# Attention and expert mixture on one core: inverse row sums of 24 spans split in two, transposed together with the row maxima one slot later, and spread to the heads' rows by a 0/1 product

## The reference, cut to what matters

```python
x = x + xattn(layernorm(x), ctx, ctx, ...)     # 16 query heads, 4 key heads, causal, 4 batches of 512 tokens
x = x + ffn(layernorm(x), ...)                 # router, top 4 of 128, 8 basis units, 2 shared units

# inside xattn
scores = einsum('bgnqd,bgkd->bgnqk', qg, k) * scale
scores = where(causal, scores, -1e30)
attn   = softmax(scores)                       # row maximum, exponential, row sum
out    = einsum('bgnqk,bgkd->bgnqd', attn, v)
```

## Time and profile before

| | |
|---|---|
| median of 3 runs | 805.96 us (805.74 to 808.08) |
| the profiled execution | 808.76 us, its span 807.0 us |
| mean granted TensorE clock over the span | 0.985 |
| TensorE busy | 764.5 us, 95% of the span |
| VectorE, ScalarE, GpSimd busy | 648.7, 575.9, 534.8 us |

### The profile page before, as it was taken

How to read it: one execution, slowest core, us unless ns; L and a number is a source line. 1 busy time by engine, 2 the same in 40 slices (tenths; PEclk the granted TensorE clock), 3 DMA queues, 4 the chain that set the end, 5 groups by cost and what they waited for, 6 DMA issues and landing times. The chain is left out here.

```text
span 807.0 us, 15292 instructions
## 1 busy us (share of the span) xinstructions
PE 764.5 (95%) x4180; PEld 607.6 (75%) x4180; DVE 648.7 (80%) x1639; ACT 575.9 (71%) x1409; POOL 534.8 (66%) x685
## 2 busy tenths in 40 slices
PE   2769799999999999999999999999999999999998
PEld 2546577777777878877778778787778887788886
DVE  7767987889788877889789787898788887688774
ACT  3878797788777867788778767787777775655552
POOL 5585689784697769775687859776565615662572
PEclk9977999999999999999999999999999999999999
DMA  8322144554545446645455445554545335454650
GB/s 292 124 67 89 42 140 162 177 168 138 194 161 173 147 141 223 191 152 180 147 174 179 141 154 181 172 166 139 199 152 172 129 127 185 157 186 132 207 203 34
DMA packets 57052, 127.03 MB, mean 157 GB/s; under 512 B 10920, under 2 KB 28040, under 8 KB 56968
## 3 DMA queue, kind: packets, MB, share of 16 engines
q1 hardware_dynamic: 56968, 126.04, 47.3%
HBM read 107.55 MB, written 4.46 MB: 139 GB/s over the span
## 5 line engine op out<-in xcount | busy, mean ns | idle before, releaser
L1656 PE MATMUL u<-w_h,t_h 128*128 128x512 f32 x640 | 257.8, 403 | 0.7 <-issue 0.5
L1656 PE MATMUL u<-w_l,t_h 128*128 128x512 f32 x640 | 250.5, 391 | 0.0
L1656 PE MATMUL u<-w_h,t_l 128*128 128x512 f32 x640 | 250.4, 391 | 0.0
L1296 DVE TENSOR_TENSOR w_l<-w_raw,w_h 128x512 fp32r<-128x512 f32 x288 | 242.3, 868 | 0.3 <-ACT w_h L956 0.3
L956 ACT ACTIVATE w_h<-w_raw 128x512 fp32r<-128x512 f32 x380 | 216.8, 621 | 8.5 <-DMA w_raw<-in_w_units 7.4
L910 POOL TENSOR_TENSOR w_l<-w_raw,w_h 128x512 fp32r<-128x512 f32 x96 | 139.4, 1452 | 96.5 <-ACT w_h L956 96.4
L991 ACT ACTIVATE scores<-scores,mx 128x384 f32<-128x384 f32 (+1 forms) x224 | 128.8, 575 | 72.9 <-DVE mx L1239 71.7
L918 POOL TENSOR_TENSOR macc<-macc,gb 128x256 f32<-128x256 f32 x112 | 106.6, 955 | 58.4 <-DVE gb L1403 58.1
L1239 DVE CUSTOM_DVE_ANT_0 scores<-s,mask_qk 128x384 f32<-128x384 f32 (+1 forms) x224 | 112.4, 503 | 35.9 <-PE s L1532 34.8
L1656 PEld LDWEIGHTS u<-w_h,t_l 128*128 128x128 f32 x640 | 120.2, 188 | 27.0
L1656 PEld LDWEIGHTS u<-w_h,t_h 128*128 128x128 f32 x640 | 120.6, 188 | 25.7 <-issue 2.7
(11 more groups left out here) (153 smaller groups left out, 1180.8 us busy)
## 6 DMA issues: line engine op xcount, KB each, us to landing
w_raw<-in_w_units SPq DMA_DIRECT2D x160, 512.0 KB, 4.2
w_raw<-in_w_out_t SPq DMA_DIRECT2D x16, 512.0 KB, 5.2
w_raw<-in_shared_w_down SPq DMA_DIRECT2D x16, 512.0 KB, 4.6
q_st<-turned_h SPq DMA_DIRECT2D x224, 32.0 KB, 2.9
out<-x SPq DMA_DIRECT2D x16, 256.0 KB, 2.3
q_st<-turned_l SPq DMA_DIRECT2D x112, 32.0 KB, 2.8
x<-in_x SPq DMA_DIRECT2D x3, 1024.0 KB, 9.2
k_st<-turned_h SPq DMA_DIRECT2D x48, 32.0 KB, 2.8
```

Source lines behind the costliest of these rows:

```text
L1296: e.tensor_tensor(w_l[:, i % WR, k, :], w_raw[:, i % WR, k, :], f32(w_h[:, i % WR, k, :]), ALU.subtract).then_inc(s_wl, 1)
L1656: last = e.matmul(u_bank[n % 2][:], t[:, k, cols], ww[:, i % WR, k, :], start=(k == 0 and m == 0), stop=(k == KC - 1 and m == 2))
```

## The change

For spans 8 to 31 the 8 inverse sums of a row are no longer copied 32 times and transposed as 128x128 blocks. GpSimd splits them into a high and a low part (two instructions on 128x8) beside the maxima's parts in `mhl`, which becomes 16 wide. `maxima_turn` then turns maxima and inverse sums together; it becomes two ordinary products in the rounded 32-bit format with the identity (for spans 4 to 7 too, maxima alone). For spans 8 to 31 it moves from the end of slot S to slot S+1, behind the first product of `pass_a`, and waits for GpSimd's split; `maxima_out` and `rows` move to S+1 too. `inverse_turn` becomes one product of 256 columns, a 128x128 matrix of zeros and ones ("chooser") times `m_t`, and moves from S+5 to S+3. GpSimd's split is the first work of its slot S+1; VectorE inverts earlier in slot S, behind the eviction of the last filler. The chooser is made once by GpSimd in slot 52, in the place that `rrep` had.

```diff
+INVERSE_ROWS, CHOOSER_SLOT, MAXIMA_LATER = 3, 52, 1
...
+    SPREAD = H * KV
...
-        mhl, m_t = sb("mhl", [P, 2, TH, 2 * G], F32R), sb("m_t", [2 * G, Q], F32R)
-        rrep, r_t = sb("rrep", [P, TH, P]), sb("r_t", [P, 2, Q])
+        mhl, m_t = sb("mhl", [P, 2, TH, 4 * G], F32R), sb("m_t", [P, Q], F32R)
+        with ExitStack() as before:
+            rrep = before.enter_context(nc.sbuf_tensor("rrep", [P, TH, P], F32))
+        chooser, r_t = sb("chooser", [P, TH, P], F32R), sb("r_t", [P, 2, Q])
...
             for u in range(KV, NU):
-                if s == span_slot(u) + CORE[name]:
+                if s == span_slot(u) + CORE[name] + (MAXIMA_LATER if name == "maxima" and u >= SPREAD else 0):
                     return u
...
-            return u if u is not None and (u < H * KV) == first else None
+            return u if u is not None and (u < SPREAD or MAXIMA_LATER > 0) == first else None
...
+        def inverse_parts(u):
+            return s_isplit, 4 + 2 * (u - SPREAD + 1)
...
+        def inverse_rows_in(s):
+            for u in range(SPREAD, NU):
+                if s == span_slot(u):
+                    return u
+            return None
+
+        def inverse_turn_in(s):
             for u in range(NU):
-                if s == span_slot(u) + core(u, name):
+                if s == span_slot(u) + (core(u, "inverse_turn") if u < SPREAD else INVERSE_ROWS):
                     return u
...
+            def inverse_split(u):
+                r = u % 2
+                hi, lo = (mhl[:, r, :, i * G:(i + 1) * G] for i in range(2))
+                e.wait_ge(s_rinv, u + 1)
+                if u >= KV + 2:
+                    e.wait_ge(s_mt, u - KV - 1)
+                e.tensor_copy(hi, rinv[:, r]).then_inc(s_isplit, 1)
+                e.wait_ge(s_isplit, inverse_parts(u)[1] - 1)
+                e.tensor_tensor(lo, rinv[:, r], f32(hi), ALU.subtract).then_inc(s_isplit, 1)
+            def make_chooser():
+                e.wait_ge(s_rt1, SPREAD)
+                rows = chooser[:, 0, :]
+                e.memset(f32(rows), 0.0).then_inc(s_isplit, 1)
...
+                e.affine_select(out=by_head(rows), in_=by_head(f32(rows)), compare_op=ALU.not_equal, fill=1.0, base=0,
...
+                e.affine_select(out=by_head(rows), in_=by_head(f32(rows)), compare_op=ALU.not_equal, fill=1.0, base=-G,
...
             for s in slots:
+                if (u := inverse_rows_in(s - 1)) is not None:
+                    inverse_split(u)
                 if (step := second_pass_step(s - SELECT)) is not None:
                     mask_probabilities(*step)
                 if (hb := of_half(s, "query_scale")) is not None:
                     query_scale(hb)
-                if (u := of_span(s, "spread")) is not None:
+                if s == CHOOSER_SLOT:
+                    make_chooser()
+                if (u := of_spread_span(s, "spread")) is not None:
                     spread_inverse(u)
...
+                if u > SPREAD:
+                    e.wait_ge(s_rt1, u)
+                made = 2 * G if u < SPREAD else 4 * G
+                e.activation(m_t[0:made, :], short("maxima", u - KV)[0:made, 0:Q], ACT.Copy).then_inc(s_mout, 1)
...
             def maxima_turn(u):
                 e.wait_ge(s_mlo, u - KV + 1)
+                if u >= SPREAD:
+                    e.wait_ge(*inverse_parts(u))
+                first = 2 * G if u < SPREAD else 0
                 e.wait_ge(*short_free("maxima", u - KV))
                 bank = short("maxima", u - KV)
                 for t in range(TH):
-                    last = e.transpose(bank[0:2 * G, t * P:(t + 1) * P], f32(mhl[:, u % 2, t, :]), ident[:])
+                    last = e.matmul(bank[0:4 * G - first, t * P:(t + 1) * P], mhl[:, u % 2, t, first:4 * G], ident_r[:],
+                                    start=True, stop=True)
                 last.then_inc(s_mt, 1)
 
             def inverse_turn(u):
 
+                if u >= SPREAD:
+                    e.wait_ge(s_mout, u - KV + 1)
+                    e.wait_ge(*short_free("inverse", u))
+                    e.matmul(short("inverse", u)[:, 0:Q], chooser[:, 0, :], m_t[:],
+                             start=True, stop=True).then_inc(s_rt1, 1)
+                    return
```

More of the change, by code:

```diff
@@ L706, in rows @@
                     e.wait_ge(*queries_read(u - QR))
+                first = 0 if u < SPREAD else 2 * G
                 for k in range(2):
                     e.dma_start(f32(q_st[MAXROW + k:MAXROW + k + 1, u % QR, :, :]),
-                                f32(m_t[k * G:(k + 1) * G, :])).then_inc(s_m[u % 2], 16)
+                                f32(m_t[first + k * G:first + (k + 1) * G, :])).then_inc(s_m[u % 2], 16)
             def store(g):
@@ L773, in pool_engine @@
             e.memset(half_neg[:], -0.5).then_inc(s_small, 1)
-            e.memset(ident[:], 0.0)
+            e.memset(f32(m_t[:]), 0.0).then_inc(s_isplit, 1)
+            e.memset(ident, 0.0)
             e.memset(lg[:, :, :, NE:NE + 8], -1.0)
@@ L982, in maxima_out @@
                     e.wait_ge(*max_rows(u - 1))
-                e.activation(m_t[:], short("maxima", u - KV)[0:2 * G, 0:Q], ACT.Copy).then_inc(s_mout, 1)
+                if u == KV:
+                    e.wait_ge(s_isplit, 1)
+                if u > SPREAD:
+                    e.wait_ge(s_rt1, u)
+                made = 2 * G if u < SPREAD else 4 * G
+                e.activation(m_t[0:made, :], short("maxima", u - KV)[0:made, 0:Q], ACT.Copy).then_inc(s_mout, 1)
             def row_sum(u, m):
@@ L1438, in vector_engine @@
                     mixture_table()
+                if (u := inverse_rows_in(s)) is not None:
+                    inverse(u)
                 for u, m in first_pass_tiles(s)[1:]:
@@ L1491, in turn_in @@
                 for t in range(TH):
-                    last = e.transpose(bank[:, t * P:(t + 1) * P], r1_b[:, n % 2, t, :], ident[:])
+                    last = e.transpose(bank[:, t * P:(t + 1) * P], r1_b[:, n % 2, t, :], ident)
                 last.then_inc(s_turn, 1)
@@ L1503, in turn_stacked @@
                             copies = r3[:, n % 2, t * G + 2 * i + j].rearrange("p c d -> p (c d)")
-                            last = e.transpose(stack_banks(n)[i][0:MAXROW, j * Q + t * P:j * Q + (t + 1) * P], copies, ident[:])
+                            last = e.transpose(stack_banks(n)[i][0:MAXROW, j * Q + t * P:j * Q + (t + 1) * P], copies, ident)
                     last.then_inc(done, 1)
@@ L1520, in inverse_turn @@
                 for t in range(TH):
-                    last = e.transpose(bank[:, t * P:(t + 1) * P], rrep[:, t, :], ident[:])
+                    last = e.transpose(bank[:, t * P:(t + 1) * P], rrep[:, t, :], ident)
                 last.then_inc(s_rt1, 1)
@@ L1542, in turn_probabilities @@
                         at = j * w + t * P - seen(u, k)
-                        last = e.transpose(pair[:, at:at + P], masked_scores(u, j * TH + t)[:, k * P:(k + 1) * P], ident[:])
+                        last = e.transpose(pair[:, at:at + P], masked_scores(u, j * TH + t)[:, k * P:(k + 1) * P], ident)
                 last.then_inc(s_pb, 1)
@@ L1579, in turn_x @@
                 for k in range(KC):
-                    last = e.transpose(bank[:, k * P:(k + 1) * P], xn[:, k * P:(k + 1) * P], ident[:])
+                    last = e.transpose(bank[:, k * P:(k + 1) * P], xn[:, k * P:(k + 1) * P], ident)
                 last.then_inc(s_xt, 1)
@@ L1599, in turn_choice @@
                 for t in range(2):
-                    last = e.transpose(bank[:, t * P:(t + 1) * P], cf[:, t, 0:NE], ident[:])
+                    last = e.transpose(bank[:, t * P:(t + 1) * P], cf[:, t, 0:NE], ident)
                 last.then_inc(s_cft, 1)
@@ L1622, in turn_down @@
                     for k in range(ND // 2):
-                        last = e.transpose(bank[:, k * P:(k + 1) * P], blocks[h * (ND // 2) + k], ident[:])
+                        last = e.transpose(bank[:, k * P:(k + 1) * P], blocks[h * (ND // 2) + k], ident)
                     last.then_inc(s_dt, 1)
```

37 lines of the change are left out of this document (25 added, 12 removed).

## The result

The changed kernel takes 846.63 us (median of six runs, 845.85 to 850.25) against 807.68 of the kernel before in the same session (six runs, 805.74 to 809.87). The ratio is 1.0484, its 95% interval 1.0466 to 1.0502. The forecast was 844, in a range of 822 to 862.

What follows compares the result with a forecast made beforehand. TensorE, without slack from about slot 56, was taken to bound the kernel: 33 us of waits + 7 clock - 2.4 work = 37.6 us, on the 805.96 median 843.6, taken as 844; own ends 831 to 862, with feedback 822 to 862.

Steps and rivals of the forecast that it cites:

- Lags read as GpSimd's arrival less TensorE's: At slot S+1 in the old trace: 4.37 us at u = 10, 18, 26; 2.68 at u = 8; split adds 0.75.
- The kind with little lag: Spans u = 9, 17, 25, 29, 31: lag -0.3 to 0 us, so each waits 0.5 to 0.75, 3.1 in all.
- No wait elsewhere: At u = 12 and nine spans (11, 15, 19, 20, 23, 27, 28, 30 among them) GpSimd's split makes TensorE wait nowhere.
- The sum of the waits: TensorE's waits for GpSimd's split in S+1: 34.3 us, less 1.3 for engines drawing nearer, taken as 33.
- Clock: Granted clock dips behind four waits of over 4 us, 1.7 us lost each: 7 us, range 0 to 14.
- TensorE's work: Inverse product saves 2.4 us over 24 spans, maxima's products no change: -2.4 us, ends -5.2 and +3.8.
- Transfers of the maxima's rows, SyncE, ScalarE: Moved at no cost: about 1.5 us of cover left at u = 31; otherwise up to 0.5 us in 24 spans.
- What the trace would show: TensorE's waits grouped under POOL, some 33 us, three of about 5; maxima's pair 0.22 us apart from what follows, chooser's product 0.12.
- Feedback: Rival: engines draw closer after each stop, only four long waits (19.7 us) stay, clock holds: 823 us; chance 0.10.
- GpSimd in time: Rival: each lag falls below -0.75 us, only TensorE's savings are left: 801 us at best; chance 0.04.
- 128-column products at 0.22: Rival: the maxima's products cost 0.22 us each, 6.2 us more, with GpSimd in time: 810 us; chance 0.03.
- A clock that stays low for twice as long: Rival: after each of eight waits, 28 us lost instead of 7, and the split costs 1.2: 872 us; chance 0.06.

Runs made afterwards that it cites:

- The wait alone: Kernel before with maxima transposes moved to S+1, which also wait there for GpSimd's old spread copy: 860.12 us, ratio 1.0652.
- the place alone: Kernel before with only the maxima's transposes, their copy and transfer moved to S+1 for spans 8 to 31: 810.55 us, ratio 1.0038.
- without GpSimd in the path: Changed kernel with the split's two instructions on VectorE, behind its reciprocal in slot S: 821.72 us, ratio 1.0171 to the kernel before.
- the restored kernel: Changed kernel with `mhl` laid out last and 128 unused bytes in its old place: 848.67 us, ratio 1.0497 to the kernel before.
- the decoupled kernel: Changed kernel with maxima alone in slot S, GpSimd's parts turned by their own products in S+3, 8-row 0/1 product in S+5: 820.41 us, ratio 1.0142.

## Why the prediction was right

The time came as forecast, 846.6 for 844, and for the reason given: TensorE waits in its slot S+1 for GpSimd, which works in order and is later there than four slots of distance had let anyone see. The experiments bear out both halves. The wait alone makes the old kernel 49.6 us slower and the place alone 3; without GpSimd in the path 25 us come back; a rotary tile moved ahead of the slot removes its share. That the number is off by less than 3 us is in part luck, since terms that were too large and too small cancel. By step:

- **TensorE has no slack.** Held. The slots' differences add up to the span's.
- **Lags read as GpSimd's arrival less TensorE's.** Held in kind for the long ones: at u = 10, 18 and 26 the starts moved by 4.4 us instead of 5.1, at u = 8 by 4.3 instead of 4.4. At u = 10 TensorE came at 172.53, GpSimd began the split at 176.37, and TensorE went on at 176.95. So the lag was 3.84 us and not 4.37, and the split with its hop 0.58 and not 0.75; most of what was too large is the lag. The 1.3 us taken off the sum for engines that draw nearer was the right kind of term for these three (1.6 us together), but most of the other lags grew.
- **The kind with little lag.** Mis-sized: 0.5 to 0.75 for u = 9, 17 and 25, measured 1.6 to 1.8 from start to start. Two things were left out. The split takes 1.27 us beside VectorE's `w_l` instructions, and the lag itself is +0.2 to +0.5 us there instead of -0.3 to 0: TensorE reaches S+1 earlier, since the maxima's pair no longer stands in slot S, while GpSimd does not. At u = 29 and 31, 0.6 and 0.7 from start to start came as forecast.
- **No wait elsewhere.** True at u = 12, 15, 20, 23, 28 and 30. At 11, 19 and 27 the pair waits 0.6 to 0.7 us for a bank that VectorE's `d_l` still reads, the very thing named as what could prove the prediction wrong; it is 1.9 us.
- **The sum of the waits.** 33 forecast. From start to start, as the forecast read them, the fifteen waits for GpSimd are 35.6 us (32.6 of idling): the long ones too large, the short ones too small. The three for VectorE's bank come on top.
- **Clock.** 7 us forecast for four stretches, up to 8.5 measured in five. The size of one, up to 1.7, was right; which stop has one isn't given by its length alone.
- **TensorE's work.** -2.4 forecast. In the slots that the change touches it is -3.2 once idling and clock are taken out (+1.8 in S+1, -5.4 in S, +3.2 in S+3, -2.8 in S+5), with slower fillers in it and, at each stop, some 0.15 us of lengthening that the idle time leaves out (4.41 us against 4.26 at u = 10). The term that was off is the maxima's products: a pair costs 0.17 and not 0.22, which makes 1.4 us, and not the 2.8 of the low end, which counted only up to the next start. The Trainium skill, page TensorE: Matmul & The Clock Gate, section Back-to-back issue gap, has 56 ns for 128 columns as an isolated gap. The 56 to 65 ns from the pair's first product to its second are close to it; the price of a pair in this stream is 0.05 us more than twice that.
- **Tile placement.** Not foreseen: 2 to 5 us in the kernel before, by moving tiles alone. It takes away about what TensorE's cheaper products gave.
- **Transfers of the maxima's rows, SyncE, ScalarE.** No wait of TensorE names them: the place alone is 3 us in all, and its waits are no larger than before.
- **What the trace would show.** Wrong in two things: the large group is named "issue", not POOL, and the maxima's pair stands 0.12 us from what follows, not 0.22.
- **Rivals.** Feedback would have left the four long stops only; the short ones stayed, 17.7 us of 34.6. GpSimd in time, and 128-column products at 0.22, are refuted by rows. A clock that stays low for twice as long (6.8 us) was seen behind three stops of the restored kernel and behind one in the kernel with the turn behind half of the filler, never in the changed kernel itself.
- **The ends of the range.** Added up as the prediction names them they give 830 to 864, not 831 to 862; the measured time is inside either.

Of the kernel with the split on VectorE, 13.1 us longer than before in its profile, 11.0 are idling, 2.5 the clock and the opening part, and -0.5 TensorE's work, in which cheaper products and slower fillers cancel. Of the decoupled kernel's 11.5 us of work, 7.0 are the new products and 4.5 are left for the fillers, where the moved tiles alone made 3.5 to 3.9. Open is the rule of placement.

## What to carry to other kernels

Before a value is awaited earlier, compare in the old trace the time at which its maker would have it with the time at which its reader would ask, at every place, not the shares of busy time: distance in slots hides an engine's lag, and an in-order engine with 34% of idle time made TensorE stand 4.4 us longer three times. Five of the six stops of over 2 us here were charged twice, the second time in clock. A short product's price includes what it delays in front of and behind itself. And where tiles are added or resized, a kernel without the change but with the same shift belongs among the experiments; here it was worth about as much as all that the change saved.

## What was not expected of the hardware

- A product over 8 rows took 0.31 us to the next start, the same one over 128 rows 0.12. It also started 0.09 us later behind the product ahead, and its weight load only began with it.
- A pair of 128-column products takes 0.12 us, but the 512-column product behind it takes 0.28 instead of 0.23.
- GpSimd's 128x8 instructions took 0.19 and 0.20 us alone and 0.65 and 0.54 beside VectorE's 128x512 one with two inputs; VectorE's own took 0.69 and 0.55 in slot S at u = 9.
- Stops of 2.14 us at u = 16 and u = 24 in like surroundings: 3.4 us at half rate at the first, none at the second.
- The place of tiles in SBUF changes 512-column matmuls on unchanged code from 389 ns to 392 or 394 (those with `w_l`), and their distance from start to start from 227 to 229 or 233.
